# A four-layer network in one kernel: the bias table of layer 2 laid beside norm and routing, and layer 3's feed-forward joined with the last block

## What is computed

```python
x = L0_attn_x                                   # 8 sequences of 512 tokens, 128 channels, float32
for n, (mixer, ffn) in enumerate(layers):       # four layers, written out one by one
    xn = _layernorm(x, axis=-1)
    s = mixer[n](xn, ...)
    g = _silu(ffn[n](xn, ...))
    x = x + s * g
...
# layer 2: mixer with a relative position bias for each of 16 heads; its feed-forward routes each token to 2 of 8 experts
values = rel_emb[rp_bucket]                     # 32 buckets, by the distance of query and key
scores = jnp.einsum('bnqd,bnkd->bnqk', q, k) + position_bias
# layer 3: causal attention with slopes; the feed-forward is dense, with integer weights
gate = jnp.einsum('bsd,hd->bsh', x, wg)         # wg, wu, wd = integers * 1/127; hidden width 384
up = jnp.einsum('bsd,hd->bsh', x, wu)
h = jax.nn.silu(gate) * up
return jnp.einsum('bsh,dh->bsd', h, wd)
```

## Time and profile before

| what | value |
|---|---|
| median of 3 runs | 2532.12 us (2523.0 to 2532.25) |
| the profiled execution: its own time / its span | 2534.29 us / 2531.9 us |
| PE, PEld busy | 81%, 52% |
| DVE, ACT, POOL busy | 59%, 46%, 18% |
| L2norm, first DMA to last logits | 677.1 to 723.4 us |
| L2route, DVE's chain | 723.8 to 741.0 us |
| spread, first to last DVE instruction | 741.6 to 796.3 us |
| t5, first matmul | 796.6 us |
| L3ffn, first matmul | 2451.1 us |
| finish, first to last instruction | 2516.7 to 2529.2 us |

### The profile page before, as it was taken

One profiled execution on the slowest core, in us unless ns is written; L12 is line 12 of the kernel. 1 busy time (PEld: TensorE's weight loads), 2 busy tenths in 40 slices (PEclk: granted clock), 3 DMA queues, 4 the chain that ended last, 5 costly groups with the idle time before them and its releaser, 6 DMA issues. The chain is left out here.

```text
span 2531.9 us, 41611 instructions
## 1 busy us (share of the span) xinstructions
PE 2049.8 (81%) x14039; PEld 1322.5 (52%) x14039; DVE 1488.8 (59%) x4128; ACT 1163.4 (46%) x2345; POOL 443.7 (18%) x522
## 2 busy tenths in 40 slices
PE   3435998459437999999999999999794388999876
PEld 3324995438434555555555555555593144444445
DVE  4675223542356767677777767677465666666434
ACT  1123553234312666666666666666231125555542
POOL 0163550054210111111110000000163100000000
PEclk9867998669758999999999999999897558888888
DMA  3413652046313000000000000001374222232001
GB/s 124 130 40 111 230 203 72 1 142 229 117 66 85 9 10 9 9 10 9 11 7 1 1 1 1 1 1 51 104 256 157 66 89 91 64 90 92 6 11 33
DMA packets 120663, 173.61 MB, mean 69 GB/s; under 512 B 16184, under 2 KB 79776, under 8 KB 120016
## 3 DMA queue, kind: packets, MB, share of 16 engines
q1 hardware_dynamic: 108448, 141.97, 17.8%
q0 software_dynamic: 11584, 23.91, 2.7%
q10 hardware_dynamic: 432, 5.19, 0.5%
HBM read 68.27 MB, written 45.40 MB: 45 GB/s over the span
## 5 line engine op out<-in xcount | busy, mean ns | idle before, releaser
L1890 ACT ACTIVATE t_p<-t_p,t_low 128x512 f32<-128x512 f32 x512 | 369.3, 721 | 333.4 <-DVE t_low L1961 333.3
L1961 DVE CUSTOM_DVE_ANT_0 t_p<-bank,L_skewed 128x512 f32<-128x512 f32 x512 | 332.6, 687 | 276.8 <-PE bank L1783 276.8
L129 PE MATMUL pair<-ident,t_p 128*128 128x128 f32 x2048 | 279.9, 280 | 0.0
L129 PEld LDWEIGHTS pair<-ident,t_p 128*128 128x128 f32 x2048 | 219.0, 141 | 94.8 <-issue 92.6
L2303 ACT ACTIVATE alibi_p<-pair 128x1024 f32<-128x1024 f32 (+1 forms) x192 | 169.0, 884 | 171.8 <-PE pair L2190 171.6
L2362 DVE CUSTOM_DVE_ANT_0 alibi_junk<-bank,alibi_later 128x512 bf16<-128x512 f32 (+1 forms) x256 | 150.7, 623 | 97.1 <-PE bank L2202 94.8
L2040 POOL COPY t_wide<-t_inverse 128x512 f32<-128x512 f32 x64 | 39.2, 612 | 913.7 <-DVE t_inverse L1977 904.8
L2202 PE MATMUL bank<-alibi_k_aug,alibi_q_aug 32*128 32x512 f32 (+1 forms) x256 | 106.1, 568 | 35.1 <-DMA alibi_k_aug<-aug_k 15.1
L1783 PEld LDWEIGHTS bank<-t_k_hi,t_q_hi 64*128 64x128 f32 x512 | 47.7, 183 | 161.6 <-issue 149.6
L1783 PE MATMUL bank<-t_k_hi,t_q_hi 64*128 64x512 f32 x512 | 127.8, 496 | 3.5 <-DVE t_low L1961 3.2
L1805 PE MATMUL pair<-t_pT,t_v 128*64 128x512 f32 x512 | 123.8, 605 | 1.5 <-DVE t_hT L1984 1.5
(11 more groups left out here) (489 smaller groups left out, 4416.7 us busy)
## 6 DMA issues: line engine op xcount, KB each, us to landing
L0moe_w<-L_packed SPq DMA_DIRECT2D x39, 578.0 KB, 3.4
L2moe_w<-L_skewed SPq DMA_DIRECT2D x39, 450.0 KB, 3.1
L1moe_w<-L_packed SPq DMA_DIRECT2D x23, 578.0 KB, 3.4
alibi_q_aug<-aug_q SPq DMA_DIRECT2D x8, 1024.0 KB, 7.7
alibi_k_aug<-aug_k SPq DMA_DIRECT2D x8, 1024.0 KB, 7.8
L_skewed<-bias_table SPq DMA_DIRECT2D x16, 448.0 KB, 9.3
slots<-g ACTq DMA_DIRECT2D x3, 1690.0 KB, 10.7
L0moe_xs<-slots SPq DMA_DIRECT2D x39, 130.0 KB, 3.3
```

The source lines that it names most:

```text
L129: last = nc.tensor.transpose(out[0:piece.shape[1], j * P:j * P + piece.shape[0]], piece, ident[0:piece.shape[0], 0:piece.shape[0]])
L1890: nc.scalar.activation(p[:, u % RING, :], p[:, u % RING, :], ACT.Exp, bias=low[:, u % 16:u % 16 + 1], scale=-1.0, accum_out=sums[:, n % 2, ...
L1961: nc.vector.tensor_tensor_reduce(out=p[:, u % RING, :], in0=score_ps[h][:], in1=skewed[:, (n % PAIRS) * 2 + h, start:start + SEQ], scale=- ...
```

## The change

`spread_bias_block` becomes a class `Bias` whose pieces are called from inside L2norm and L2route:

- L2norm: DVE first makes the 31 copies (`lay_out`), then its own work, and `sum_slopes` ahead of the root. SP stores the table after two gathers (`write`), issues the other six, then the 16 loads (`load`; each head now has a semaphore of its own) and, when all rows are filled, the four stores of the constant rows (`store_rows`). POOL runs `make`. PE makes 8 flips (EARLY = 8, heads 0 to 3, three banks in turn) ahead of its transposes. ACT moves these 8 back, between its silus and the root, and fills the four constant rows at its end (both were DVE's work).
- L2route: PE makes six more flips, then the ranking, then the last 18, six banks in turn; ACT moves all 24, behind the exp. POOL waits for the four stores.
- The block `spread` is gone.

`experts_block` and `finish_block` become `quantized_ffn_block`: the weights are read where they are, DVE cuts them first and x one sequence at a time, the way down of chunk n - 2 follows the way up of chunk n, the last silu is taken from PSUM, and product, sum and store of a sequence follow inside the loop. `retire_block` now comes behind it, as the last block of the program. Layer 2 clears 15 semaphores more, layer 3 two fewer.

```diff
 def norm_block(..., bias=None):
...
                         gather(k, sp, b, 1, tiles(k.g, b).unsqueeze(2))
+                    if bias and b == 1:
+                        bias.write(sp)
+                if bias:
+                    bias.load(sp)
+                    bias.store_rows(sp)
...
                     nc.scalar.activation(gate[:, b % RING], tiles(k.g, b), ACT.Silu).then_inc(gated, 1)
+            if bias:
+                for n in range(bias.EARLY):
+                    bias.move(act, n, flip_ps[n % 3])
             act.wait_ge(collected, NB)
             nc.scalar.activation(root[:], mv[:, :, 1], ACT.Sqrt, bias=k.eps[:]).then_inc(rooted, 1)
...
+            if bias:
+                bias.fill_rows(act)
...
+            if bias:
+                for n in range(bias.EARLY):
+                    bias.turn(pe, n, flip_ps[n % 3], n - 2 if n >= 3 else None)
             for b in range(NB):
                 turn_rows(b)
...
 def route_block(..., table=None):
+            free = k.banks[2:8]
+            late = range(table.EARLY, 2 * HEADS) if table else range(0)
+            for j, n in enumerate(late):
+                if j == len(free):
+                    rank(pe)
+                table.turn(pe, n, free[j % len(free)], n - len(free) + 1 if j >= len(free) else None)
...
                 nc.scalar.activation(big[1][:], big[1][:], ACT.Exp).then_inc(act_s, 1)
+            if table:
+                for j, n in enumerate(range(table.EARLY, 2 * HEADS)):
+                    table.move(act, n, k.banks[2 + j % 6])
...
+    def turn(self, pe, n, bank, before):
+        if n == 0:
+            pe.wait_ge(self.flip_made, 2)
+        if before is not None:
+            pe.wait_ge(self.moved, before)
+        pe.wait_ge(self.read[n // 2], 16)
+        self.k.nc.tensor.matmul(bank[:, 0:self.HALF], self.flip[:], self.place(n), start=True, stop=True).then_inc(self.flipped, 1)
...
+def quantized_ffn_block(k, name, chunks, turned):
...
+            for n in range(N):
+                up_chunk(n)
+                if n >= 2:
+                    down_chunk(n - 2)
+            down_chunk(N - 2)
+            down_chunk(N - 1)
...
+            def finish(b):
+                act.wait_ge(down, (b + 1) * chunks)
+                if b >= 2:
+                    act.wait_ge(scaled, b - 1)
+                nc.scalar.activation(last[:, b % 2], down_ps[b % 2][:].rearrange("p (t d) -> p t d", d=P), ACT.Silu).then_inc(silu, 1)
...
         run(3, layer3)
-        finish_block(k)
```

More of the change, by code:

```diff
@@ L322, in _ @@
                         gather(k, sp, b, 1, tiles(k.g, b).unsqueeze(2))
+                    if bias and b == 1:
[4 more added lines that the diff above has]
+        if bias:
+            @block.gpsimd
+            def _(pool):
+                bias.make(pool)
         def xn(b, t):
@@ L441, in _, with route_block @@
                 route(NB - 1)
[L444 to L485, removed]
+def route_block(k, name, logits, bias, top, kind, rows, layer, table=None):
     nc, T, E = k.nc, k.NT, EXPERTS
@@ L522, in _ @@
                            allow_small_or_imprecise_dtypes=True).then_inc(made, 1)
+            if table:
+                pool.wait_ge(table.steady_stored, 64)
         @block.vector
@@ L612, in _ @@
             nc.tensor.matmul(total[:, 0:E * T], k.ones[:], flat(chosen), start=True, stop=True).then_inc(ranked, 1)
+        @block.tensor
+        def _(pe):
+            free = k.banks[2:8]
[4 more added lines that the diff above has]
+                table.turn(pe, n, free[j % len(free)], n - len(free) + 1 if j >= len(free) else None)
+            if not table:
+                rank(pe)
         @block.scalar
@@ L913, in _ @@
                     ins.then_inc(summed if j else half_sum, 1)
-def experts_block(k, name, chunks, func, loads, n_routed=0, last=None, weights=None, gated=False, biased=True):
+def quantized_ffn_block(k, name, chunks, turned):
     nc, NB = k.nc, k.NB
+    N = NB * chunks
     with ExitStack() as ctx:
         st = Stage(k, name, ctx)
[L923 to L952, removed]
-        block = ctx.enter_context(nc.Block())
[L954 to L976, removed]
@@ new lines, in _, with place_x @@
+        @block.scalar
+        def _(act):
+            def place_x(b):
+                act.wait_ge(x_cut_s, b + 1)
+                if b >= 2:
+                    act.wait_ge(up, (b - 1) * chunks)
+                nc.scalar.copy(x_high[:, b % 2, :], x_cut[:, b % 2, :]).then_inc(x_high_s, 1)
+            def finish(b):
+                act.wait_ge(down, (b + 1) * chunks)
+                if b >= 2:
+                    act.wait_ge(scaled, b - 1)
+                nc.scalar.activation(last[:, b % 2], down_ps[b % 2][:].rearrange("p (t d) -> p t d", d=P), ACT.Silu).then_inc(silu, 1)
+            act.wait_ge(w_cut_s, 1)
+            nc.scalar.copy(w_high[:], w_cut[:]).then_inc(w_high_s, 1)
+            place_x(0)
+            for n in range(N):
+                b, c = n // chunks, n % chunks
+                act.wait_ge(up, n + 1)
+                if n >= 2:
+                    act.wait_ge(hidden, n - 1)
+                nc.scalar.activation(gate[:, n % 2, :], up_ps[n % 2 * 2 + 1][:], ACT.Silu).then_inc(gated, 1)
+                if c == 0 and b + 1 < NB:
+                    place_x(b + 1)
+                if c == 2 and b >= 1:
+                    finish(b - 1)
+            finish(NB - 1)
@@ new lines, in _, with cut, cut_x, scale @@
+        @block.vector
+        def _(dve):
+            V = nc.vector
+            def cut(out, src):
+                return V.tensor_scalar(out.bitcast(I32), src.bitcast(I32), KEEP_12_BITS, None, ALU.bitwise_and)
+            def cut_x(b):
+                if b >= 2:
+                    dve.wait_ge(x_high_s, b - 1)
+                    dve.wait_ge(x_low_s, b - 1)
+                cut(x_cut[:, b % 2, :], cols(k.xnT, b)).then_inc(x_cut_s, 1)
+                dve.wait_ge(x_cut_s, b + 1)
+                if b >= 2:
+                    dve.wait_ge(up, (b - 1) * chunks)
+                V.tensor_tensor(x_low[:, b % 2, :], cols(k.xnT, b), x_cut[:, b % 2, :], ALU.subtract).then_inc(x_low_s, 1)
+            def scale(b):
+                dve.wait_ge(silu, b + 1)
+                V.tensor_tensor(tiles(k.s, b), tiles(k.s, b), last[:, b % 2], ALU.mult).then_inc(scaled, 1)
+            def add(b):
+                dve.wait_ge(scaled, b + 1)
+                V.tensor_tensor(tiles(k.x, b), tiles(k.x, b), tiles(k.s, b), ALU.add).then_inc(added, 1)
+            for side in range(2):
+                ins = cut(w_cut[:, side], turned[:, 1 - side])
+            ins.then_inc(w_cut_s, 1)
+            cut_x(0)
+            dve.wait_ge(w_cut_s, 1)
+            for side in range(2):
+                ins = V.tensor_tensor(w_low[:, side], turned[:, 1 - side], w_cut[:, side], ALU.subtract)
+            ins.then_inc(w_low_s, 1)
+            for n in range(N):
+                b, c = n // chunks, n % chunks
+                dve.wait_ge(gated, n + 1)
+                if b >= 2:
+                    dve.wait_ge(down, n - 2 * chunks + 1)
+                V.tensor_tensor(hT[:, b % 2, c, :], up_ps[n % 2 * 2][:], gate[:, n % 2, :], ALU.mult).then_inc(hidden, 1)
+                if c == 0 and b + 1 < NB:
+                    cut_x(b + 1)
+                if c == 0 and b >= 2:
+                    scale(b - 2)
+                if c == 1 and b >= 2:
+                    add(b - 2)
+            for b in range(NB - 2, NB):
+                scale(b)
+                add(b)
@@ L978, in _ @@
         @block.sync
         def _(sp):
[L980 to L1004, removed]
@@ L1160, in build_kernel @@
+            for b in range(NB):
+                sp.wait_ge(added, b + 1)
+                sp.dma_start(dst[:, b * TPS:(b + 1) * TPS, :], k.x[:, b * TPS:(b + 1) * TPS, :]).then_inc(out_s, 16)
+            sp.wait_ge(out_s, 16 * NB)
 def build_kernel(nc, inputs, out):
```

331 lines of the change are left out of this document (120 added, 211 removed).

## The result

The changed kernel takes 2476.16 us (median of 4 runs, 2463.91 to 2482.65), the kernel before beside it 2532.18 us (2523.0 to 2545.82). The ratio is 0.9758, interval 0.9721 to 0.9795. Forecast were 2470 us, 2461 to 2487.

The account below looks back on a forecast made before the run. Blocks stand in a row, each bound by its last engine; `spread` took 55.5 us. Gains of 42.3 us in layer 2 and 20.4 in layer 3, 62.7 off 2534.29, less 2.2 to the median, gave 2470 us, range 2461 to 2487.

Parts of the forecast that it names:

- not faster: Rival, 3%: t5 stays long at half clock after broken flips; 125 us of it cancels the gain, 150 gives 2545 us.
- the band comes late: Rival, 10%: L2norm's band loads queue on SP, first head near 700, root and all behind 10 us late, 2480 us.
- More is gained: Rival, 22%: stores hold SP only 1.6 us, clock still up in L2norm or at layer 3's start; 2464 us, or 2461.
- Gathers and loads: L2norm: later gathers cost nothing, up to 2.5 us uncovered; loads give the first flip at 690, between 686 and 693.
- Root: L2norm: eight flips, ACT's copies and the table load put the root at 700.9 instead of 699.99, +0.9 us.
- Stores: End of L2norm: SP's issue of four constant-row stores takes 5.15 us; route's DVE begins 5.4 us later in all.
- Flips at full clock: L2route: 18 flips behind the exp at 0.76 us each, 13.7 us; t5 begins at 753.1 instead of 796.57.
- half clock: Rival, 15%: the flips stay at half clock, costing 13.1 us, up to 17 with the early ones; 2483 to 2487 us.
- POOL beside DVE: L2norm: POOL's constants beside DVE's work cost nothing, as 0.9 us of cover precedes the root; other bound 5 us.
- Start: Layer 3's feed-forward: weights cut first, uncopied, put the first matmul at 2443.2 instead of 2451.07, 7.8 us gained.
- Loop: Layer 3's feed-forward: new order covers PE's 3.3 us of waits for DVE's product; 1.5 us gained, between nothing and 3.3.
- End: Layer 3: last way down to last sum 2.2 us instead of 18.5, less 5.2 for the retire behind it; 11.1 us gained.

Follow-up runs that it names:

- run 5: The changed kernel measured again on another chip, with not a line changed: 2467.6 us, ratio 0.9755.
- run 7: The changed kernel with the four stores issued in L2route, four ACT copies before the exp with nine flips before the ranking, no last retire: 2456.0 us, ratio 0.9711.
- run 3: The changed kernel with SP issuing the four constant-row stores at the start of L2route, not the end of L2norm: 2467.82 us, ratio 0.974.
- run 1: The changed kernel with layer 3's old feed-forward and last block put back, so layer 2's change alone: 2493.49 us, ratio 0.9859.
- run 6: The changed kernel without the last block, which clears layer 3's semaphores at the program's end: 2463.57 us, ratio 0.9747.
- run 8: The changed kernel with layer 3's way down for a sequence again behind all three of its chunks up: 2488.28 us, one execution.
- run 9: The changed kernel with no early flips in L2norm (EARLY = 0), all 32 in L2route: 2470.11 us, one execution.
- run 4: The changed kernel with four of ACT's copies ahead of the exp and nine flips instead of six ahead of the ranking: 2469.12 us, ratio 0.9748.

## Why the prediction was right, and which terms were off

**Layer 2, forecast 42.3 us, measured 39.6** (78.75 instead of 119.44, less 1.1 for the clears: from DVE's last copy in t5 to the next layer's weights 6.3 us instead of 5.2). t5 begins close behind the last copy, as forecast, and its own length up to its last copy is the same 993.9 us (1.6 more in runs 5 and 7, where the clock fell in it); the rival "not faster" falls, as does "the band comes late". "More is gained" falls too: the stores held SP 5.1 us, and the clock stood at half in L2norm's transposes and at layer 3's first matmul.

- *Gathers and loads.* The first flip came at 693.3, at the end of the range and not at the 690 that I took. In run 5 it came 14.2 us behind the first gather, in the first profile 15.5, so this moves by a us from one execution to the next. The first load landed 7.2 us behind its issue at 685.99, and 2.9 us behind the last gather; before, with no gathers ahead, it took 4.1 us, and about that I took.
- *Root.* Said was +0.9 us; it is 2.5 (25.3 instead of 22.9 us behind the gather), and 1.5 in run 5. The step that failed is the first flip's time; the chain behind it held, with ACT's copies of 0.53 us and a clock that rose after 3.5 us, not 5.4. Of the 2.5 us 0.5 are DVE's (below). Of the drain that the Trainium skill (ScalarE: Activation LUTs, What ACT_TABLE_LOAD costs) adds, to about 2.66 us, nothing shows: the root starts 1.29 us behind the load's start.
- *Stores.* Said were 5.2 us of SP's issue holding the next block; it is 0.79 + 4.32 us, and run 3 took 4.3 of them away by moving the issue. This was the largest cost of the change, and it was seen.
- *Flips at full clock.* Right behind the exp, 0.75 us each. Not foreseen was the fall of the clock from 741.1 to 744.6, which cost 1.7 us: from that row of flips to t5's first matmul it is 16.4 us, in run 5 14.7, and the row itself 4.97 instead of 3.27. The rival "half clock" had the mechanism, at 13 us for the whole phase; it came for an eighth of that, and in four of the five profiles with this code in layer 2 (after, runs 1, 6 and 8; not in run 5).
- *POOL beside DVE.* The 31 copies took 4.15 us, not 3.35, and the first product came 0.6 us later (4.1 instead of 3.5 us behind the gather). POOL worked beside them both times; what made them slower no run separates. Named were 0.9 us of cover: run 9's root, with no copies on ACT ahead of it, stood 23.4 us behind the gather instead of 22.9, so 0.5 us came through, where I took nothing.

**Layer 3, forecast 20.4 us, measured 23.2.** Start 7.9 (said 7.8), with the clock at half as before. Loop 3.4 (said 1.5, between nothing and 3.3): the clock rose after 3.4 us instead of 5.7, worth 1.2, and the other 2.1 are the new block's, where the wait of 3.3 us went to 0.2 as seen in the weight loads' row. Runs 5 and 6, in which the clock rose after 5.8 and 5.6 us, took 57.6 and 57.5 us: 2.0 and 2.1 less than before, with no help of the clock. I had sized it too low; run 8 shows what the order prevents, 3.5 to 3.7 us in a block that has more for DVE to do. End 16.4 - 4.5 = 11.9 (said 11.1): the retire added 4.5, not the 5.2 of before's row, and the last steps took 2.1. Why the retire is shorter at the program's end no run shows.

**The sum.** 39.6 + 23.2 - 0.7 (a later start) + 0.3 (between the clears and L3norm) = 62.4, forecast 62.7: the terms that were off, -2.7 in layer 2 and +2.8 in layer 3, cancel. This is luck in part. In run 5 it is alike: 40.9 us from layer 2's first gather to L3norm's, and 7.9 + 2.0 + 16.4 - 4.5 = 21.8 in layer 3. By medians the gain is 56.0 us in the first measurement and 63.9 in the second; both intervals (52 to 71 and 56 to 68) hold the forecast.

**What is left is not the change.** Eleven profiles (before, after and the nine runs), in all of which these instructions are the same, show L3norm's first gather to attention's last sum in 485 to 514 us. The stretch from a point 125 us behind the gather to that last sum, in the columns of the earlier trace rows, first after:

```profile
2028.10:2393.58 365.48, 327.95 (x4372) 169.16 (x4369) 211.49 (x769) 198.77 (x258) 15.30 (x12) 0.87 0.21 65
```
Run 6:
```profile
2027.40:2387.50 360.10, 320.87 (x4372) 167.48 (x4370) 211.50 (x769) 198.42 (x258) 15.31 (x12) 0.89 0.21 66
```
Run 8:
```profile
2025.30:2413.88 388.58, 351.41 (x4369) 179.92 (x4368) 210.65 (x767) 198.87 (x258) 15.29 (x12) 0.80 0.19 61
```

DVE, ACT and POOL are busy for the same time in each; only PE's time moves, with its granted clock (a few matmul records are missing in run 8): 360 us at 0.89, 365 at 0.87, 389 at 0.80. Before it was 372.8 us at 0.85: the 7.3 us of the table above. The two profiled executions of the changed kernel differ by 10.2 us, and by 11.6 in attention (run 5's stretch: 377.1 us at 0.83). So it is likely also what spreads the runs of one kernel over 7 to 23 us; only one execution of each set was profiled. Why the clock falls more often in one execution than in another was not found out.

## What to carry to other kernels

Work may go beside another block's chain for little (of the 55.5 us of `spread` 40.7 are gone), but what an engine only issues also holds the block's end: the four stores on SP cost 4.3 us at a seam where every other engine was done, and moving that one call gave them back. Ask of each moved copy which table load or root stands behind it on its engine. And where a change is worth a few us, compare stretches between marks in the trace, and see first how far a stretch with no edit in it differs. Put the last mark behind the next long stretch too: a fall of the clock that an edit seems to avoid may only come later.

## What the runs showed of the hardware

- **The clock around a short idle.** PE's row in L2route is: six flips, an idle time ahead of the ranking, two small matmuls, 0.6 us idle, then flips again. In four executions the idle time was 1.59 to 1.71 us, and the clock fell to 0.50 within the next flips (in the first profile eight matmuls then took 4.97 us). In three it was 0.95 to 1.52 us, in two more there was none, and the clock stayed up there (3.27 us where the row is the same). The idle is longer where the clock had risen sooner in the six flips ahead. But the idle alone does not decide: at t5's begin PE has the same idle times in all eleven executions (0.6, 0.3 and 1.4 us in its first 6.4 us), and the clock fell behind them in two, runs 5 and 7, both of which had kept it at the ranking, as runs 3, 4 and 9 had too. What decides stays open.
- **Flips raised the clock, the turns behind them did not.** Eight flips ended at 701.3 at clock 1.00; it fell to 0.50 at 703.6, while PE was idle until its first transpose at 706.0. From 705.0 to 723.4 PE was then busy 17.4 of 18.4 us at 0.50. The Trainium skill (TensorE: Matmul & The Clock Gate, Part 4: PE-mode transpose) says that transposes do not count as busy in the same way, which this agrees with; no run separated them from the small router matmuls between.
- **Stores from 16 partitions.** Of four stores of 256 KB the first two held SP 0.79 us together, the last two 4.32. That this is the same in all eleven executions, at other places and beside other work, fits a cost of the issue itself; no run changed their shape.
